# Layer norm in token rows: statistics during the scan, one VectorE pass per quad at the end

## Chip, core and metric

The kernel runs on one core of a Trainium2 chip. The metric is device microseconds (us) of one execution; the time of a kernel is the median of its runs.

## What is computed

B = 32 sequences of T = 64 tokens with D = 512 features, in float32. A GRU runs over the tokens (its first state is `cond`) and is added to x; then a layer takes sums of 8 tokens as blocks (8 per sequence), scores and mixes them, projects the mix, adds it to every token and normalises; the result is added once more.

```
h_t = gru_cell(h_{t-1}, x_t);          x1 = x + h            # 64 steps in sequence
block_n = sum of x1 over 8 tokens;     keys = block_n @ Wk^T, scaled to unit rms, * rms_weight
attn = softmax(keys . q);              att = sum_n attn_n * block_n      # one row per sequence
proj = att @ Wo^T;                     u = x1 + proj
out = x1 + (u - mean(u)) / sqrt(var(u) + eps) * gamma + beta
```

## The kernel before

Layouts. "Recurrence layout": partition = 32 j + b, with j a quarter of the features (128 columns) and b the sequence; a tile [128, 128] is one token of all sequences. A quad is 4 tokens; there are 16. Five instruction streams are written out by hand, one per engine, ordered by semaphores.

Start. SP loads the biases, the first quad of x, then `w_ih` and `w_hh` in four pieces each, each piece after an earlier one has landed. TensorE adds the first four tokens' input products into four PSUM banks as pieces land.

Scan, 64 steps: the first 8 and the last 8 written out, the rest in a hardware loop of 8. A step: 16 recurrent products (L618), each 32 stationary columns into its own 32 partitions; ScalarE's sigmoid (L475) and two tanh (L484); VectorE's cell (L839 to L760), which ends in three transpositions into `h_t` that TensorE's next product waits for. TensorE meanwhile runs the input chunk for five steps ahead (`gi_chunk`, L581), which VectorE takes out (`keep_gi`, L738) and an SP transfer (`move_gi`, L240) brings into recurrence layout; ScalarE lays it into PSUM for the next step (L444). At step 2 of a quad ScalarE and VectorE split the next x into two parts (`split_x`). Behind the cell VectorE does the quad's share: `quad_sum` (x1 = x + h, L768), `quad_partial_sums`, `quad_centre` with TensorE's mean (L604, L778) into `cx_all`, `quad_steps_sum`, and per block `block_sum`. GpSimd adds beta to x1 into `xb_all` (L366). In the last 8 steps there are no chunks from step 59 on; TensorE makes the keys of blocks 0 to 6, SP loads the constants (`load_consts`, L254) and VectorE waits for them at step 60 (L887).

After the scan: scores, softmax, last block's key, and the projection `cp` (centred, one row per sequence, L970). Then the end: `cp` is added to all of `cx_all` (by VectorE L1030, GpSimd L401, and for the last quads by TensorE into PSUM, L701, L702), ScalarE and VectorE square and sum (L534, L976), TensorE sums over the four quarters (L710), the root is refined in five small operations (`refine`), `scale` multiplies by root and gamma (L1009), GpSimd and VectorE add `xb_all` (L406, L1058), SP stores (L320).

## Time and profile before

| | us |
|---|---|
| median of 3 runs | 402.81 (401.72 to 405.34) |
| profiled execution, its time | 404.12 |
| its span, first to last instruction | 402.3 |
| mean granted TensorE clock | 0.961 |

The profile is of one execution. Its page gives busy time by engine and the costliest groups; further views are windows (busy time of each engine in a stretch), the chain of waits (what released each piece of the work that ended last) and timelines. Busy times of TensorE are modelled ends of pipelined products.

### The profile page before, as it was taken

To read this page: it belongs to the slowest core of one execution; us is meant where nothing else is said; L and a number is where in the kernel's file an instruction comes from. 1 tells how busy PE (TensorE), PEld (TensorE's weight loads), DVE (VectorE), ACT (ScalarE), POOL (GpSimd) and SP (SyncE) were. 2 spreads that over 40 slices of the span, in tenths; PEclk is the share of its full clock that TensorE was granted. 3 is DMA by queue.
4 is the path that set the end of the run, shared out by engine and by line. 5 is a ranking of instruction groups with operands and counts; after the bars stand their busy time and mean duration, and the time that the engine had idled before them with its cause. 6 is when DMAs were issued, how large, how long until landed. Compare 5 with 4: busy or idle time off the path is not lost.

```text
span 402.3 us, 9322 instructions
## 1 busy us (share of the span) xinstructions
PE 359.9 (89%) x3102; PEld 212.6 (53%) x3102; DVE 287.7 (72%) x1192; ACT 136.0 (34%) x494; POOL 59.5 (15%) x69
## 2 busy tenths in 40 slices
PE   7999999999999999999999999999999997856300
PEld 4545656565656565656565656565656532623100
DVE  2626767776777677767776777677767667799997
ACT  4502232323232323232323232323234543446532
POOL 3012101010101010101010101010101010263563
PEclk9999999999999999999999999999999999896955
DMA  6956525222222222222222222222221230000234
GB/s 231 399 215 134 174 64 170 66 69 65 66 63 67 62 66 63 67 62 66 63 67 62 66 63 67 63 65 63 67 63 42 65 93 26 2 0 1 104 157 156
DMA packets 18368, 35.46 MB, mean 88 GB/s; under 512 B 1940, under 2 KB 10652, under 8 KB 18348
## 3 DMA queue, kind: packets, MB, share of 16 engines
q1 hardware_dynamic: 18268, 35.15, 29.3%
q8 instruction: 10, 0.16, 0.2%
q0 software_dynamic: 80, 0.07, 0.1%
q14 instruction: 10, 0.08, 0.1%
HBM read 19.21 MB, written 4.19 MB: 58 GB/s over the span
## 4 chain that ended last, share of the span: by engine, by line
PE 73%; DVE 15%; DMA 8%; SPq 1%; issue 1%; POOL 1%; ACT 0%; DVEq 0%; POOLq 0%
PE gates_ps L618 38%; PE gi_ps L581 32%; DVE cx_all L1009 5%; DMA xb_all<-in_w_ih_dram 3%; DVE cx_all L1030 2%; DMA w_hh<-in_w_hh_dram 2%; DMA gamma<-in_gamma_dram 2%; DMA cx_all<-in_b_hh_dram 1%; DVE cx_all L1058 1%; PE third_ps L682 1%; PE third_ps L618 1%; DVE w_hh L1001 1%; PE fourth_ps L618 1%; DVE w_hh L995 1%; DVE cx_all L1025 1%
## 5 line engine op out<-in xcount | busy, mean ns | idle before, releaser
L618 PE MATMUL gates_ps<-w_hh,h_t 128*32 128x384 f32 x1920 | 167.3, 489 | 2.4 <-DVE h_t L760 2.1
L618 PEld LDWEIGHTS gates_ps<-w_hh,h_t 128*32 128x32 f32 x1920 | 56.7, 109 | 84.5 <-issue 54.4
L581 PE MATMUL gi_ps<-w_ih_hi,xt_hi 128*128 128x384 f32 x240 | 86.8, 362 | 0.0
L475 ACT ACTIVATE rz<-gates_ps 128x256 f32<-128x256 f32 x60 | 23.0, 384 | 171.3 <-PE gates_ps L618 171.3
L581 PE MATMUL gi_ps<-w_ih_lo,xt_hi 128*128 128x384 f32 x240 | 80.9, 337 | 0.0
L581 PE MATMUL gi_ps<-w_ih_hi,xt_lo 128*128 128x384 f32 x240 | 80.7, 336 | 0.0
L839 DVE TENSOR_TENSOR rz<-gates_ps,rz 128x128 f32<-128x128 f32 x60 | 17.5, 292 | 80.2 <-ACT rz L475 80.2
L581 PEld LDWEIGHTS gi_ps<-w_ih_hi,xt_hi 128*128 128x128 f32 x240 | 45.0, 188 | 37.5 <-issue 36.8
L366 POOL TENSOR_TENSOR xb_all<-x,beta 128x512 f32 (+1 forms) x16 | 21.2, 1322 | 175.9 <-DVE x L768 175.9
L581 PEld LDWEIGHTS gi_ps<-w_ih_lo,xt_hi 128*128 128x128 f32 x240 | 45.1, 188 | 0.0
L581 PEld LDWEIGHTS gi_ps<-w_ih_hi,xt_lo 128*128 128x128 f32 x240 | 45.1, 188 | 0.0
L760 DVE STREAM_TRANSPOSE h_t<-hist 128x32 f32<-128x32 f32 x189 | 36.5, 217 | 2.4 <-issue 0.2
L754 DVE TENSOR_TENSOR hist<-zh,n 128x32 f32<-128x32 f32 (+1 forms) x192 | 34.2, 201 | 2.2
L738 DVE TENSOR_TENSOR gi_tok<-gi_ps,b_in 128x384 f32<-128x384 f32 x60 | 33.1, 551 | 2.0 <-POOL b_in L380 1.5
L747 DVE SCALAR_TENSOR_TENSOR n<-rz,n 128x32 f32<-128x32 f32 (+1 forms) x192 | 31.0, 189 | 0.0
L484 ACT ACTIVATE n<-n 128x32 f32<-128x32 f32 (+1 forms) x128 | 28.9, 256 | 3.8 <-DVE n L844 3.8
L435 ACT ACTIVATE gates_ps<-bhh_n 128x128 f32<-128x128 f32 x60 | 16.9, 281 | 21.5 <-DVE rz L839 21.5
L444 ACT ACTIVATE gates_ps<-gi 128x256 f32<-128x256 f32 x60 | 22.5, 375 | 1.9 <-DMA gi<-gi_tok 0.3
L844 DVE TENSOR_TENSOR n<-rz,gi 128x32 f32<-128x32 f32 x120 | 21.6, 222 | 0.0
L406 POOL TENSOR_TENSOR cx_all<-cx_all,xb_all 128x1024 f32<-128x1024 f32 x7 | 17.5, 2501 | 16.4 <-DVE cx_all L1009 15.4
L372 POOL COPY br_all<-br_cur 128x128 f32 x7 | 2.0, 289 | 100.0 <-DVE br_turned L792 100.0
L784 DVE TENSOR_REDUCE bs<-x 128x128 f32<-128x512 f32 x15 | 16.1, 1074 | 0.0
(197 smaller groups left out, 332.7 us busy)
## 6 DMA issues: line engine op xcount, KB each, us to landing
gi<-gi_tok SPq DMA_DIRECT2D x60, 192.0 KB, 3.3
x<-in_x_rec_dram SPq DMA_DIRECT2D x16, 256.0 KB, 2.8
x_t<-in_x_t_dram SPq DMA_DIRECT2D x15, 256.0 KB, 3.2
out_dram<-cx_all SPq DMA_DIRECT2D x7, 512.0 KB, 2.6
xb_all<-in_w_ih_dram SPq DMA_DIRECT2D x4, 768.0 KB, 6.9
w_hh<-in_w_hh_dram SPq DMA_DIRECT2D x4, 768.0 KB, 7.9
wo_t<-in_wo_t_dram SPq DMA_DIRECT2D x1, 1024.0 KB, 5.4
wk_t<-in_wk_t_dram SPq DMA_DIRECT2D x1, 1024.0 KB, 5.5
```

The lines of the kernel that those rows point to most:

```text
L366: pool.tensor_tensor(xb_all[:, bass.ds(quad * Q, Q), :], x1[:], over_steps(beta), ALU.add).then_inc(xb_ready, 1)
L444: act.activation(gates_ps[:, P:3 * P], gi[:, (s // Q) % 2, first + P:first + G3], ACT.Copy).then_inc(seeded, 1)
L475: act.activation(rz[:], gates_bank(t)[:, P:3 * P], ACT.Sigmoid).then_inc(rz_ready, 1)
L484: act.activation(n[:, c], n[:, c], ACT.Tanh).then_inc(n_ready, 1)
L581: mm = pe.matmul(gi_ps[tok][:, 0:G3], a[:, k, :], w[:, k, gi_cols(j)], start=(k == 0 and a is xt_hi and w is w_ih_hi), stop=(k == NJ - 1 a ...
L618: mm = pe.matmul(gates_bank(t)[j * B:(j + 1) * B, P:], h_t[:, k * B:(k + 1) * B], chunk(w_hh, k, j), start=False, stop=(k == NJ - 1), skip ...
L738: dve.tensor_tensor(gi_tok[:, tok, :], gi_ps[tok][:, 0:G3], b_in[:, gi_cols(j)], ALU.add).then_inc(gi_tok_ready, 1)
L747: dve.scalar_tensor_tensor(out=n[:, c], in0=z[:, c], scalar=1.0, in1=n[:, c], op0=ALU.subtract, op1=ALU.mult).then_inc(terms_ready, 1)
L754: dve.tensor_tensor(hist[:, s, c], zh[:, c], n[:, c], ALU.subtract).then_inc(h_ready, 1)
L760: dve.transpose(h_t[:, c], hist[:, s, c]).then_inc(ht_ready, 1)
L844: dve.tensor_tensor(n[:, c], r[:, c], i_n[:, c], ALU.add).then_inc(n_pre_ready[number], 1)
L1009: ins = dve.scalar_tensor_tensor(out=cx_all[:, c * C + t, :], in0=u_of(c, t), scalar=rstd[:, c * C + t:c * C + t + 1], in1=gamma[:], op0=A ...
```

## The change

x1 is kept twice: feature-major in `x1t` [feature, quad, 4, (b, step)], as x arrives for the input products, with the turned state added in place; and token-major in `gcx` [(b, step), quad, 512], where the state comes through `h_tok`, four SP transfers a quad from `hist`. With a token's 512 features in one row, ScalarE takes its mean and its sum of squares with accumulators at step 2 of a quad (`token_stats`), VectorE centres and multiplies by gamma (`centre_tokens`); ScalarE adds beta to `x1t` (`add_beta`). The variance of u = x1 + cp is s2 + 2 x1.cp + |cp|^2: after `cp` TensorE makes the middle term for all tokens (`cross_sums`), VectorE picks each token's own sequence, GpSimd raises to the power -0.5, TensorE lays the root out by token. TensorE transposes x1 + beta of each quad into a PSUM bank (`lay_x1`) and adds root times gamma times cp (`add_gcp`, 32 contraction rows each, by quad another 32 rows of the array); VectorE's `finish` is gcx * root + bank, and SP stores each quad. GpSimd's beta add, TensorE's quad mean, the squares, `refine`, `scale` and the adds of `cp` and x go. Constants are loaded at the start through the ScalarE queue and spread by TensorE (`lay_pick`). `score_keys` moves into the last cell. The last block is summed in turned form.

The core of the diff, blank lines left out:

```diff
+        keys_wq, b_of_tok, last_hs, last_part = b_in[:, 0:D], b_in[:, D:D + P], b_in[:, D + P:D + 2 * P], b_in[:, D + 2 * P:D + 3 * P]
+        gmask = b_in[:, 2 * D:3 * D].rearrange("p (j u) -> p j u", j=NJ)
...
+            def move_h(quad, slot, j):
+                if j == 0:
+                    wait(sp, x1t_ready, quad + 1)
+                    wait(sp, x1_ready, quad)
+                sp.dma_start(h_tok[:, j * P:(j + 1) * P], hist[j * B:(j + 1) * B, slot * Q:(slot + 1) * Q, :]
+                             ).then_inc(h_tok_in, 16)
...
                     if not (last and i * S + s + 5 >= T):
                         move_gi(i, s)
-                    if last and s == 2:
-                        load_consts()
+                    if s % Q == Q - 1 and not (last and s == S - 1):
+                        for j in range(NJ):
+                            move_h(i * 2 + s // Q, s // Q, j)
             def load_w_ih(k):
...
             load_w_ih(0)
             sp.dma_start(hist[:, S - 1, :], cond_d).then_inc(h0_in, 16)
             load_w_ih(1)
             load_w_ih(2)
+            load_w_ih(3)
+            load_x_t(1)
             sp.wait_ge(w_ih_in[0], 16)
-            load_w_ih(3)
-            load_ahead(1)
+            load_w_hh(0)
             sp.wait_ge(w_ih_in[1], 16)
-            load_w_hh(0)
+            load_w_hh(1)
             sp.wait_ge(w_ih_in[2], 16)
-            load_w_hh(1)
+            load_w_hh(2)
             sp.wait_ge(w_ih_in[3], 16)
-            load_w_hh(2)
...
+            for j in range(NJ):
+                if j == 0:
+                    sp.wait_ge(h_ready, 3 * T)
+                    sp.wait_ge(x1_ready, NQ - 1)
+                sp.dma_start(h_tok[:, j * P:(j + 1) * P], hist[j * B:(j + 1) * B, Q:S, :]).then_inc(h_tok_in, 16)
+            for quad in range(NQ):
+                sp.wait_ge(out_ready, quad + 1)
+                sp.dma_start(out[:, quad, :], gcx[:, quad, :]).then_inc(out_stored, 16)
...
-            pool.wait_ge(cp_ready, 1)
-            for c in (2, 3, 5):
-                v = cx_all[:, c * S:(c + 1) * S, :]
-                pool.tensor_tensor(v, v, over_steps(cp, S), ALU.add).then_inc(u_pool, 1)
-            for c in range(NB - 1):
-                pool.wait_ge(scaled, c + 1)
-                v = cx_all[:, c * S:(c + 1) * S, :]
-                pool.tensor_tensor(v, v, xb_all[:, c * S:(c + 1) * S, :], ALU.add).then_inc(out_pool, 1)
+            for part, owns in enumerate(parts_i):
+                cols = slice(owns[0] * Q, (owns[-1] + 1) * Q)
+                pool.wait_ge(var_ready, part + 1)
+                pool.tensor_tensor(rstd[:, cols], var[:, cols], half[:, 0:Q * len(owns)], ALU.pow
+                                   ).then_inc(rstd_ready, 1)
...
+            def token_stats(quad, trash=third_ps[:]):
+                wait(act, x1_ready, quad + 1)
+                act.activation(trash, gcx_of(quad), ACT.Copy, scale=-1.0 / D, accum_out=column(x_mean, quad)
+                               ).then_inc(mean_ready, 1)
+                wait(act, mean_ready, quad + 1)
+                act.activation(trash, gcx_of(quad), ACT.Square, bias=column(x_mean, quad),
+                               accum_out=column(s2_tok, quad)).then_inc(s2_ready, 1)
+            def add_beta(quad):
+                if isinstance(quad, int) and quad == NQ - 1:
+                    act.wait_ge(pre_step, 1)
+                else:
+                    wait(act, part_ready, quad + 1)
+                tile = x1t_of(quad)
+                for k in range(NJ):
+                    ins = act.activation(tile[:, k, :], tile[:, k, :], ACT.Identity,
+                                         bias=beta_t[:, k * B:k * B + 1])
+                ins.then_inc(beta_added, 1)
...
+            act.wait_ge(cp_ready, 1)
+            act.wait_ge(last_sq_ready, 1)
+            act.activation(cp_sq, cp, ACT.Square, accum_out=cp_sums[:, 0:1]).then_inc(cp_squared, 1)
+            act.wait_ge(gcp_laid, 1)
+            act.activation(gcp_all, gates_ps[:], ACT.Copy).then_inc(gcp_kept, 1)
+            token_stats(NQ - 1, stats_trash)
+            for part, owns in enumerate(parts_i):
+                cols = slice(owns[0] * Q, (owns[-1] + 1) * Q)
+                if part == 1:
+                    act.wait_ge(s2_laid, 2)
+                    move_s2(NQ - Q, Q, fourth_ps, 4 * Q)
+                act.wait_ge(rstd_laid, part + 1)
+                act.activation(rstd_tok[:, cols], fourth_ps[:, P + owns[0] * Q:P + (owns[-1] + 1) * Q],
+                               ACT.Copy).then_inc(rstd_kept, 1)
...
+                if first and s == 0:
+                    lay_pick(small_ps, 2)
...
+            def lay_x1(quad):
+                bank = out_ps[quad % len(out_ps)]
+                if quad == NQ - 1:
+                    pe.wait_ge(x1t_ready, NQ)
+                if quad >= len(out_ps):
+                    pe.wait_ge(out_ready, quad - len(out_ps) + 1)
+                elif bank is gates_ps:
+                    pe.wait_ge(gcp_kept, 1)
+                elif bank is cross_ps[1]:
+                    pe.wait_ge(cross_step, 4)
+                v = bank[:].rearrange("p (j k u) -> p k j u", j=NJ, k=NJ)
+                for k in range(NJ):
+                    pe.matmul(v[:, k], x1t[:, quad, k, :], ident[:], is_transpose=True, start=(k == 0), stop=False,
+                              skip_group_check=True)
...
+            def cross_sums(part, i):
+                bank, col = cross_ps[part], parts_i[part].index(i) * P
+                for k in range(NJ):
+                    for g in range(Q):
+                        mm = pe.matmul(bank[g * B:(g + 1) * B, col:col + P], cp_t[:, k * B:(k + 1) * B],
+                                       x1t[:, i * Q + g, k, :], start=(k == 0), stop=(k == NJ - 1),
+                                       skip_group_check=True)
+                if i == parts_i[part][-1]:
+                    mm.then_inc(cross_laid, 1)
+            def lay_rstd(part):
+                pe.wait_ge(rstd_spread, part + 1)
+                for i in parts_i[part]:
+                    mm = pe.matmul(fourth_ps[:, P + i * Q:P + (i + 1) * Q], rstd_of[:, i * P:(i + 1) * P],
+                                   own_n[:], start=True, stop=True, skip_group_check=True)
+                mm.then_inc(rstd_laid, 1)
+            def add_gcp(i):
+                pe.wait_ge(gcp_kept, 1)
+                for g in range(Q):
+                    rows = slice(g * B, (g + 1) * B)
+                    pe.matmul(out_ps[(i * Q + g) % len(out_ps)][:], rstd_of[rows, i * P:(i + 1) * P],
+                              gcp_all[rows, :], start=False, stop=True, skip_group_check=True,
+                              tile_position=(g * B, 0)).then_inc(u_laid, 1)
+            pe.wait_ge(cp_t_ready, 1)
+            cross_sums(0, 0)
+            pe.wait_ge(cp_squared, 1)
+            pe.wait_ge(cp_beta_ready, 1)
+            pe.matmul(fourth_ps[:, 0:2], same_b[:], cp_sums, start=True, stop=True).then_inc(cp_summed, 1)
+            pe.wait_ge(gcp_ready, 1)
+            pe.matmul(gates_ps[:], same_b[:], gcp_own, start=True, stop=True).then_inc(gcp_laid, 1)
+            cross_sums(1, 1)
+            pe.wait_ge(cp_const_ready, 1)
+            lay_rstd(0)
+            add_gcp(0)
+            pe.wait_ge(s2_split, 2)
+            pe.wait_ge(rstd_kept, 1)
+            lay_s2(NQ - Q, Q, fourth_ps, 4 * Q)
+            pe.wait_ge(cross_step, 2)
+            pe.wait_ge(x1t_ready, NQ)
+            cross_sums(2, 2)
+            cross_sums(2, 3)
+            for quad in range(Q, 2 * Q):
+                lay_x1(quad)
+            pe.wait_ge(s2_moved, 2)
+            lay_rstd(1)
+            add_gcp(1)
+            pe.wait_ge(rstd_kept, 2)
+            lay_rstd(2)
+            for i in (2, 3):
+                for g in range(Q):
+                    lay_x1(i * Q + g)
+                add_gcp(i)
         @block.vector
         def _(dve):
             def split_x(quad):
                 wait(dve, x_hi_ready, quad)
-                dve.tensor_tensor(xt_lo[:], x_t[:], xt_hi[:].bitcast(F32), ALU.subtract).then_inc(x_lo_ready, 1)
+                dve.tensor_tensor(xt_lo[:], x1t_of(quad), xt_hi[:].bitcast(F32), ALU.subtract).then_inc(x_lo_ready, 1)
             def keep_gi(idx, pos):
...
-                dve.transpose(h_t[:, c], hist[:, s, c]).then_inc(ht_ready, 1)
...
+            def add_turned(quad, slot):
+                wait(dve, ht_ready, quad * (3 * Q) + 3 * Q + 3)
+                tile = x1t_of(quad).rearrange("p k (b t) -> p (k b) t", t=Q)
+                dve.tensor_tensor(tile, tile, turned[:, slot * Q:(slot + 1) * Q, :].rearrange("p t c -> p c t"),
+                                  ALU.add).then_inc(x1t_ready, 1)
+            def sum_steps(quad, slot):
+                dve.tensor_reduce(parts_t[:, slot, :], x1t_of(quad).rearrange("p k (b t) -> p (k b) t", t=Q), AX.X,
+                                  ALU.add).then_inc(part_ready, 1)
+            def add_tokens(quad):
+                wait(dve, x_tok_in, (quad + 1) * 16)
+                wait(dve, h_tok_in, (quad + 1) * (16 * NJ))
+                dve.tensor_tensor(gcx_of(quad), gcx_of(quad), h_tok[:], ALU.add).then_inc(x1_ready, 1)
+            def centre_tokens(quad):
+                wait(dve, s2_ready, quad + 1)
+                dve.scalar_tensor_tensor(out=gcx_of(quad), in0=gcx_of(quad), scalar=column(x_mean, quad),
+                                         in1=gamma_tok[:], op0=ALU.add, op1=ALU.mult).then_inc(gcx_ready, 1)
...
+                if last and s == S - 1:
+                    score_keys()
...
                 if not (last and t + 5 >= T):
                     keep_gi(t + 5, s + 5)
                 if tt == 2 and not last:
                     split_x(quad + 2)
-                if peeled and s < 3:
+                if tt == Q - 1:
+                    add_turned(quad, slot)
...
+                if tt == 0:
+                    sum_steps(quad - 1, 1 - slot)
+                if tt == 1:
+                    add_tokens(quad - 1)
+                if tt == 2 and slot == 0:
                     block_sum(i - 1)
+                if tt == Q - 1:
+                    centre_tokens(quad - 1)
+                if last and s == 3:
+                    dve.tensor_reduce(step_of_tok[:], ident[:].rearrange("p (b t) -> p t b", t=Q), AX.X, ALU.add
+                                      ).then_inc(step_made, 1)
                 if last and s == 4:
-                    dve.wait_ge(consts_in, 16 * 5)
-                    dve.tensor_tensor(wq[:], wq[:], q_row, ALU.mult).then_inc(wq_ready, 1)
-                    dve.tensor_tensor(wq_rec[:], wq_rec[:], q_row_rec, ALU.mult).then_inc(wq_ready, 1)
+                    dve.tensor_reduce(last_part, x1t[:, NQ - 1].rearrange("p k (b t) -> p (k b) t", t=Q), AX.X,
+                                      ALU.add).then_inc(pre_step, 1)
+                    split_s2(0, NQ - Q)
                 if last and s == 5:
...
                 if last and s == 6:
-                    sum_ahead()
-                    score_keys()
...
-                dve.wait_ge(scaled, NB + number)
-                dve.tensor_tensor(v, v, xb_all[:, steps, :], ALU.add).then_inc(out_dve, 1)
+            dve.transpose(cp_t, cp).then_inc(cp_t_ready, 1)
+            dve.tensor_tensor_reduce(cp_beta, cp, beta_rec, -2.0, 0.0, ALU.mult, ALU.add, cp_sums[:, 1:2]
+                                     ).then_inc(cp_beta_ready, 1)
+            dve.wait_ge(gmask_made, 1)
+            dve.tensor_tensor(gcp_own.rearrange("p (j u) -> p j u", j=NJ), gmask,
+                              cp[:, None, :].broadcast_to([P, NJ, P]), ALU.mult).then_inc(gcp_ready, 1)
...
+            def cross_part(part):
+                owns = parts_i[part]
+                cols = slice(owns[0] * Q, (owns[-1] + 1) * Q)
+                size = len(owns)
+                own = cross_own[:, 0:size * P]
+                dve.wait_ge(cross_laid, part + 1)
+                wait(dve, cross_step, 2 * part)
+                dve.tensor_tensor(own.rearrange("p (i c) -> p i c", i=size),
+                                  cross_ps[part][:, 0:size * P].rearrange("p (i c) -> p i c", i=size),
+                                  tok_of_b[:, None, :].broadcast_to([P, size, P]), ALU.mult).then_inc(cross_step, 1)
+                dve.wait_ge(cross_step, 2 * part + 1)
+                dve.tensor_reduce(cross[:, cols].rearrange("p (i t) -> p i t", i=size),
+                                  own.rearrange("p (i b t) -> p i t b", i=size, t=Q), AX.X, ALU.add
+                                  ).then_inc(cross_step, 1)
+                dve.wait_ge(cross_step, 2 * part + 2)
+                dve.wait_ge(s2c_ready, min(part, 1) + 1)
+                dve.scalar_tensor_tensor(out=var[:, cols], in0=cross[:, cols], scalar=2.0 / D, in1=s2c[:, cols],
+                                         op0=ALU.mult, op1=ALU.add).then_inc(var_ready, 1)
+            def spread_rstd(part):
+                owns = parts_i[part]
+                cols = slice(owns[0] * Q, (owns[-1] + 1) * Q)
+                size = len(owns)
+                dve.wait_ge(rstd_ready, part + 1)
+                dve.tensor_tensor(rstd_of[:, owns[0] * P:(owns[-1] + 1) * P].rearrange("p (i b t) -> p i b t", i=size, t=Q),
+                                  tok_of_b[:].rearrange("p (b t) -> p b t", t=Q)[:, None].broadcast_to([P, size, B, Q]),
+                                  rstd[:, cols].rearrange("p (i t) -> p i t", i=size)[:, :, None].broadcast_to([P, size, B, Q]),
+                                  ALU.mult).then_inc(rstd_spread, 1)
+            def finish(quad):
+                dve.wait_ge(gcx_ready, quad + 1)
+                dve.wait_ge(u_laid, quad + 1)
+                dve.wait_ge(rstd_kept, (1, 2, 3, 3)[quad // Q])
+                dve.scalar_tensor_tensor(out=gcx[:, quad, :], in0=gcx[:, quad, :], scalar=rstd_tok[:, quad:quad + 1],
+                                         in1=out_ps[quad % len(out_ps)][:], op0=ALU.mult, op1=ALU.add
+                                         ).then_inc(out_ready, 1)
...
+            add_const(0, Q)
+            cross_part(0)
+            centre_tokens(NQ - 2)
+            spread_rstd(0)
+            centre_tokens(NQ - 1)
+            split_s2(NQ - Q, NQ)
+            for quad in range(2):
+                finish(quad)
+            dve.wait_ge(s2_moved, 2)
+            add_const(Q, NQ)
+            cross_part(1)
+            finish(2)
+            spread_rstd(1)
+            finish(3)
+            cross_part(2)
+            finish(4)
+            spread_rstd(2)
+            for quad in range(5, NQ):
+                finish(quad)
 def kernel(**inputs):
```

## Rows read from the trace of the kernel before

**Rows 1.** Page, part 1: busy us of each engine (share) xinstructions.

```profile
PE 359.9 (89%) x3102; PEld 212.6 (53%) x3102; DVE 287.7 (72%) x1192; ACT 136.0 (34%) x494; POOL 59.5 (15%) x69
```

**Rows 2.** Windows: stage, its us, busy of each engine (xcount), PE clock, DMA share, GB/s.

```profile
0.00:27.36 27.36, 23.98 (x199) 13.50 (x199) 11.36 (x24) 10.70 (x14) 3.81 (x22) 1.00 0.80 308
27.36:319.65 292.29, 292.14 (x2581) 177.62 (x2580) 207.06 (x955) 90.00 (x310) 24.61 (x31) 1.00 0.28 74
319.65:347.60 27.95, 23.91 (x190) 10.31 (x190) 19.51 (x95) 11.14 (x32) 2.56 (x4) 0.99 0.15 44
...
355.60:402.30 46.70, 14.22 (x32) 6.84 (x32) 43.59 (x106) 20.67 (x125) 25.86 (x10) 0.70 0.23 90
```

**Rows 3.** Chain of waits in the scan: start us, us, what.

```profile
57.82 2.72 PE gates_ps L618 x32
...
62.83 2.72 PE gates_ps L618 x32
...
67.95 2.72 PE gates_ps L618 x32
```

**Rows 4.** Timeline, scan, VectorE and ScalarE: start, us, instruction [idle before <-releaser].

```profile
197.04 0.29 DVE L839 TENSOR_TENSOR rz<-gates_ps,rz 128x128 f32<-128x128 f32 x1 [1.28 <-ACT rz L475]
...
207.05 0.29 DVE L839 TENSOR_TENSOR rz<-gates_ps,rz 128x128 f32<-128x128 f32 x1 [0.95 <-ACT rz L475]
...
201.63 0.38 ACT L475 ACTIVATE rz<-gates_ps 128x256 f32<-128x256 f32 x1 [2.12 <-PE gates_ps L618]
...
314.74 0.61 ACT L458 ACTIVATE wo_t<-wo_t 128x512 f32<-128x512 f32 x1
```

**Rows 5.** Timeline of the last steps: TensorE, VectorE, ScalarE.

```profile
336.05 2.79 PE L618 MATMUL gates_ps<-w_hh,h_t 128*32 128x384 f32 x32 [1.94 <-DVE h_t L760]
...
344.94 0.16 DVE L826 TENSOR_TENSOR score<-key_dot,key_rms 128x2 f32<-128x2 f32 x1 [0.79 <-POOL key_rms L393]
...
343.78 0.38 ACT L475 ACTIVATE rz<-gates_ps 128x256 f32<-128x256 f32 x1 [2.33 <-PE gates_ps L618]
```

**Rows 6.** Timeline from the last block's turned sum to cp: VectorE, GpSimd, VectorE.

```profile
347.30 0.31 DVE L928 STREAM_TRANSPOSE br_turned<-br_cur 128x128 f32<-128x128 f32 x1
...
352.74 0.56 POOL L396 TENSOR_TENSOR w_hh<-w_hh,half 128x1 f32<-128x1 f32 x1 [2.27 <-DVE w_hh L945]
...
355.29 0.29 DVE L970 TENSOR_SCALAR w_hh<-w_hh 128x128 f32<-128x128 f32 x1
```

**Rows 7.** Groups by line: out<-in xcount | busy us, mean ns | idle before.

```profile
L1030 DVE TENSOR_TENSOR cx_all<-cx_all,w_hh 128x512 f32<-128x512 f32 x4 | 8.9, 2296 | 0.0
...
L778 DVE SCALAR_TENSOR_TENSOR cx_all<-small_ps,x 128x512 f32 (+1 forms) x16 | 10.8, 677 | 0.0
```

**Rows 8.** Chain of waits, start and one later transfer issue on SP.

```profile
1.06 0.50 DVE xb_all L903
...
1.57 0.39 SPq L290
...
320.61 0.55 SPq L240
```

**Rows 9.** Timeline of TensorE after the last block.

```profile
352.99 1.08 PE L675 MATMUL gi_ps<-wo_t,w_hh 128*32 128x128 f32 x32 [0.53 <-DVE w_hh L948]
...
357.52 1.02 PE L701 MATMUL third_ps<-cx_all,ident 128*128 128x512 f32 x2
...
358.37 1.02 PE L702 MATMUL third_ps<-w_hh,ident 128*128 128x512 f32 x2
...
366.10 0.58 PE L710 MATMUL small_ps<-w_hh,same_b 128*128 128x16 f32 x2 [6.71 <-DVE w_hh L976]
...
366.52 2.06 PE L701 MATMUL gi_ps<-cx_all,ident 128*128 128x512 f32 x2
```

**Rows 10.** Page, part 6: DMA issues xcount, KB each, median us to landing.

```profile
gi<-gi_tok SPq DMA_DIRECT2D x60, 192.0 KB, 3.3
```

**Rows 11.** Timeline of VectorE, its last instruction.

```profile
399.08 0.69 DVE L1058 TENSOR_TENSOR cx_all<-cx_all,xb_all 128x512 f32<-128x512 f32 x1
```

669 lines of the change are left out of this document (288 added, 381 removed).

## Prediction

> **What bounds the kernel now.** I read the page first: TensorE is busy for 359.9 us (89% of the span), VectorE for 287.7 [rows 1]. A share over the whole span mixes stages, so the windows come next [rows 2]. There are five. A start of 27.4 us with the DMA engines 80% busy; 292 us of scan in which TensorE is never idle; 28 us of last steps; 8 us in which the attention comes down to one projection `cp`; and 46.7 us of layer norm in which VectorE is busy for 43.6 and TensorE for 14.2. The change rewrites the last stage and moves work from it into the second.
>
> The scan's period is TensorE's own. In the chain of waits a recurrent product (2.72) and an input chunk (the rest) follow each other, 5.01 from product to product, and 5.12 where the mean of a quad (L604) is laid between them [rows 3]. VectorE waits 1.28 us for the sigmoid in one step of a quad, 0.95 us in its fullest one, and ScalarE waits 2.12 us for the gates after `split_x` [rows 4]. These gaps are what the added work must fit into.
>
> In the last steps two gaps open: TensorE waits 1.94 us for a state that is late because VectorE and ScalarE stood before constants that the SP queue loads late, and VectorE waits 0.79 us for GpSimd's power before the last cell [rows 5]. From the last block's turned sum (347.61) to `cp` (355.58) it is 8.0 us [rows 6]. The end is VectorE's chain: it begins with four adds of `cp` at 2.30 us each while GpSimd adds beside it, where the same size of pass costs 0.68 in L778, with GpSimd mostly quiet [rows 7]; squares, roots, scalings and the adds of x follow it, step by step.
>
> **Removed and added, in order of time.**
>
> *Start.* One more memset (0.50, less 0.08 of overlap with its neighbour) precedes `bias_made`, and SP issues one more small load first (its neighbour takes 0.39; I take 0.35, an estimate) [rows 8]. DMA sets this stage, so all weights land 0.8 us later. w_ih 3 and w_hh 0 to 2 are issued sooner, but the last, w_hh 3, still waits for w_ih 3: I credit nothing, at best 1.3 us. The constants' products on TensorE (some 2 us) lie under those loads. `lay_pick(small_ps, 2)` does not: it stands after the first step's input chunk, four float32 products of 128 columns, a quarter of 0.85 each [rows 9], 0.85 together. Some 0.2 us that the second step waits behind `b_in` go, as the load of `b_hh` shrinks by a third. Sum +1.4.
>
> *Scan.* `quad_mean` goes from TensorE: (5.12 - 5.01) x 14 = -1.5. VectorE gets, by step of the quad, the steps' sum, the token add, nothing new, and the turned add plus centring (0.68 for each pass of 512 columns, as L778 [rows 7]): the sizes that it had, in another order, so it keeps about 1 us of gap. ScalarE gets two passes over 512 columns with accumulators (0.61 each [rows 4], some 0.3 for the read-out and the wait between them: 1.5, an estimate) in the gap of 2.12, and four bias adds of 128 columns, about 1.1, in a gap of 3 us. What is queued behind `token_stats` is the sigmoid, so its margin is 0.6 us, the smallest there is. GpSimd loses its add of beta. SP issues four more transfers (`move_h`) a quad behind the chunk move of step 3. They wait for `add_turned`, then 4 x 0.55 to issue [rows 8] and 3.3 to land [rows 10], 5.5 in all; `add_tokens` needs them two steps (10 us) later and the `hist` rows are overwritten a quad later. Nothing stalls by these numbers. The price if ScalarE's work runs over: 15 quads times what exceeds 0.6 us.
>
> *Last steps.* Constants are there from the start: -1.9. `score_keys` now stands inside the last cell, behind the adds it once held up: the sigmoid of the last cell ended at 344.16, but VectorE took the scores from 344.94 on and two operations of 0.17 first [rows 5], so -1.1, and +0.35 for these two. The last block is summed already turned: the last state must be turned first, +0.5 (an estimate: three pieces of a quarter to half of the 0.31 us block [rows 6]), and the block's own transposition goes, -0.3. ScalarE carries `square_keys`, `token_stats` and four copies of `s2` before the last sigmoid; that fits with no margin, I add 0.2. End of the turned sum: 347.6 + 1.4 - 1.5 - 1.9 - 1.1 + 0.35 + 0.5 - 0.3 + 0.2 = 345.2; with 0.4 for TensorE's first eight transpositions ahead of the keys, 345.6.
>
> *To `cp`.* The multiply over seven blocks and the reduction behind it become seven operations of 0.30 (as [rows 6] has for 128 columns); that takes work off VectorE but puts `add_tokens(15)` on the path, which waits for four transfers issued from about 344.5 on (2.2 + 3.3: 350.0). I keep 7.3 of the 8.0 us: `cp` at 352.9.
>
> *From `cp` to the first `finish`.* VectorE: turn (0.31), product with beta (0.3), `gcp_own` over 512 columns (0.68), three small ones and a cross part from PSUM (1.4), GpSimd's power (0.56, [rows 6]), the spread (0.3). TensorE in between: 16 column-strip products (1.08 for such a set), a 512-column one (1.02), 16 more, the laid root, the first `add_gcp` [rows 9]. With about 0.06 for each hand-over the chain is 5.9 us: 358.8.
>
> *The sixteen `finish` passes.* Each reads one SBUF tile and one PSUM bank over 512 columns, L778's form: 0.68 busy, about 0.62 apart [rows 7], so 9.9, and 2.8 for the cross parts, spreads and `add_const` between them: 12.7 if VectorE sets it. TensorE has per quad four transpositions, 128 columns each. No row shows one. As full float32 products they cost 4 x 0.21 = 0.85 (a quarter of 0.85 each); if each also waits for its own weights more, I bound it by 1.4, and if a transposition streams faster less, 0.4. I take 0.8; and per four quads one `add_gcp`. Its four products of 512 columns read different rows of the array. One takes 0.85 [rows 9]. The nearest row for shared strips is L618: sixteen products of 384 columns in 2.72 us [rows 3], 0.17 each where one alone streams for about 0.64 (0.85 x 384/512), so four run together. Those are column strips; row strips are in no row. So 0.9 or 3.4; I take 0.9, as that is the row nearest in kind. Then six PSUM banks couple the engines: `lay_x1(15)` waits for `finish(9)`, then transposition, `add_gcp` and four passes follow. Walking it gives the last pass 12.7 to 17.7 us after the first start; I take 15.6. Last pass ends at 374.4.
>
> The store adds what lay between the last pass (399.77) and the end, 2.5 [rows 2, 11]: span 376.9. The profiled execution of before took 404.12 us for its 402.3 us span, 1.8 more, and lies 1.3 over the runs' median of 402.81. So the forecast is 376.9 + 1.8 - 1.3 = 377.4, I say 377 us, 26 us less.
>
> The Trainium skill (TensorEngine Tiling (Array Packing), Key Properties) says that tiles operate independently, row tiles as well as column tiles. By it the four products cost about 0.9, the value taken above; no row here shows it for row tiles.
>
> **Rivals.**
> *A, the forecast* (0.52): VectorE and TensorE share the pace at the end; 371 to 382.
> *B, the row strips take turns* (0.12). For it: no row shows them together. Against: L618's strips. Each `add_gcp` costs 3.4, +2.5 four times: 387. Then the edit's claim, one VectorE pass per quad as the price, is not met: TensorE sets the end.
> *C, the clock falls* (0.12). In the last stage of before the granted clock is 0.70, and a 512-column product that took 1.02 us at the full 2.4 GHz took 2.06 after 6.7 us in which TensorE was idle [rows 2, 9]. The new end keeps TensorE at work, which speaks against it. If half of its 16 us run at 1.2 GHz: +8, 385.
> The Trainium skill (TensorE: Matmul & The Clock Gate, Part 4) says that transpositions do not count as busy for the clock. By it the stretch of 12 quads' transpositions would run at the lower level, which is rival C; no row here has a transposition on TensorE.
> *D, ScalarE's statistics hold up the scan a little* (0.14): over by 0.4 us a quad, 15 x 0.4 = 6: 383.
> *E, better than summed* (0.07): w_hh lands 1.3 sooner and transpositions hide: 371 or less.
> *F, slower than before* (0.03). One mechanism: `token_stats` stands ahead of the sigmoid of step 3. From 0.6 + 26/15 = 2.3 us over its price of 1.5 it eats the whole gain; a pass would have to cost 1.9 us instead of 0.61. At 2.5 us a pass, 15 x (5.1 - 2.1) = 45: 422. No row has such a price.
>
> The range must leave out 2 in 10: 369 to 388 leaves out F, the tail of E and of C. A measurement of this kernel can tell about 1% from no change, so faster means under 398.8. Only F and the rest of D ends there: faster 0.96, same 0.02, slower 0.02.
>
> **What would show it.** Right: the recurrent product and chunk still 5.01 apart, without the 5.12; no 1.94 us gap before the second-last step; `cp` near 353; sixteen passes of 0.68 on VectorE; four `add_gcp` products starting within 0.1 us of each other; last pass near 374. Wrong: a sigmoid that starts over 0.1 us after its gates in step 3 of a quad (D, F); `add_gcp` products 0.85 apart (B); granted clock under 0.9 after `cp` (C); first recurrent product of the second step not at 29.0.

## The result, and the profile of the changed kernel

The changed kernel takes 383.3 us (median of 4 runs, 381.33 to 385.01), the kernel before 402.9 beside it: a ratio of 0.950, interval 0.944 to 0.957, so 5% faster. The forecast was 377 us, range 369 to 388.

The page of the changed kernel, and its windows over the same five stages as before [rows 2]: start, scan, last steps, to `cp`, end.

```profile
PE 363.2 (95%) x3281; PEld 213.9 (56%) x3281; DVE 261.8 (69%) x1134; ACT 159.3 (42%) x506; POOL 20.2 (5%) x53
```

```profile
core 0: us, PE busy (x) PEld busy (x) DVE busy (x) ACT busy (x) POOL busy (x), PEclk, DMA share, GB/s
0.00:28.10 28.10, 25.68 (x211) 15.29 (x211) 12.51 (x28) 11.49 (x16) 7.89 (x30) 1.00 0.76 293
28.10:319.34 291.24, 291.24 (x2557) 173.21 (x2560) 206.50 (x951) 124.92 (x415) 5.42 (x16) 1.00 0.33 86
319.34:344.98 25.64, 23.28 (x190) 9.33 (x190) 18.73 (x94) 18.39 (x57) 2.24 (x4) 1.00 0.11 29
344.98:352.39 7.41, 4.47 (x106) 3.56 (x106) 6.35 (x24) 0.93 (x5) 0.57 (x1) 1.00 0.17 38
352.39:380.50 28.11, 18.53 (x222) 12.48 (x222) 17.74 (x39) 3.61 (x14) 4.10 (x3) 0.88 0.40 151
```

The two profiled spans differ by 21.8 us (402.3 and 380.5). By stage, from the events that bound them in both (they differ by up to 0.1 us from the round windows above): start +0.8, scan -1.1, last steps -2.2, to `cp` -0.7, end -18.6 (46.7 before, 28.1 now). VectorE was busy for 43.6 us of the end and is now for 17.7.

The end in detail. TensorE's timeline of the changed kernel, around the third root; the four products of one `add_gcp` are the lines of 32*128, here the first half of each:

```profile
363.47 0.60 PE L683 MATMUL third_ps<-ident,x1t 128*128 128x128 f32 x4
364.24 0.69 PE L740 MATMUL gates_ps<-w_hh 32*128 32x512 f32 x1
364.25 0.69 PE L740 MATMUL gi_ps<-w_hh 32*128 32x512 f32 x1
364.26 0.69 PE L740 MATMUL first_ps<-w_hh 32*128 32x512 f32 x1
364.26 0.69 PE L740 MATMUL third_ps<-w_hh 32*128 32x512 f32 x1
...
367.97 0.58 PE L731 MATMUL fourth_ps<-own_n,w_hh 128*128 128x4 f32 x4 [2.58 <-DVE w_hh L1080]
368.40 0.63 PE L683 MATMUL small_ps<-ident,x1t 128*128 128x128 f32 x4
```

GpSimd's powers and, on VectorE, what waits for them and for TensorE:

```profile
356.61 1.46 POOL L367 TENSOR_TENSOR w_hh<-w_hh,half 128x4 f32<-128x4 f32 x1 [7.03 <-DVE w_hh L1071]
362.48 1.01 POOL L367 TENSOR_TENSOR w_hh<-w_hh,half 128x4 f32<-128x4 f32 x1 [4.41 <-DVE w_hh L1071]
365.72 1.64 POOL L367 TENSOR_TENSOR w_hh<-w_hh,half 128x8 f32<-128x8 f32 x1 [2.24 <-DVE w_hh L1071]
```

```profile
360.04 0.75 DVE L1090 SCALAR_TENSOR_TENSOR gcx<-gcx,w_hh,first_ps 128x512 f32<-128x512 f32 x1 [0.31 <-issue]
...
367.39 0.42 DVE L1080 TENSOR_TENSOR w_hh<-tok_of_b,w_hh 128x256 f32<-128x256 f32 x1 [1.06 <-POOL w_hh L367]
...
371.49 0.75 DVE L1090 SCALAR_TENSOR_TENSOR gcx<-gcx,w_hh,small_ps 128x512 f32<-128x512 f32 x1 [1.70 <-issue]
...
376.80 0.74 DVE L1090 SCALAR_TENSOR_TENSOR gcx<-gcx,w_hh,gi_ps 128x512 f32<-128x512 f32 x1
```

Read them together: the root of the last eight quads is ready only at 367.4; TensorE stands still for 2.58 us in front of `lay_rstd(2)`, with transpositions queued behind it that need no root; and VectorE pays 1.70 us of that before `finish(8)`. Between the first pass and the end of the last lie 17.5 us, of which the passes themselves are 16 x 0.66 = 10.6.

### The profile page after: what moved, and what is told of

The parts are those of the page before. It is cut to its first block, busy times and chain, and to the rows that moved or that the text cites. A ratio compares the mean times of both kernels' runs of the same rounds, so it can differ in the third digit from the quotient of the medians.

```text
span 380.5 us, 9825 instructions
## 1 busy us (share of the span) xinstructions
PE 363.2 (95%) x3281; PEld 213.9 (56%) x3281; DVE 261.8 (69%) x1134; ACT 159.3 (42%) x506; POOL 20.2 (5%) x53
## 4 chain that ended last, share of the span: by engine, by line
PE 89%; DVE 5%; issue 2%; DMA 1%; POOL 1%; SPq 1%; POOLq 0%; ACT 0%; DVEq 0%
PE gates_ps L595 42%; PE gi_ps L563 36%; DMA h_tok<-hist 1%; DVE gcx L1090 1%; PE first_ps L595 1%; PE first_ps L656 1%; PE fourth_ps L595 1%; PE third_ps L595 1%; PE keys_ps L595 1%; PE fourth_ps L656 1%; PE third_ps L656 1%; PE keys_ps L656 1%; POOL w_hh L367 1%; PE gi_ps L577 0%; PE keys_ps L721 0%
## 5 line engine op out<-in xcount | busy, mean ns | idle before, releaser
L595 PE MATMUL gates_ps<-w_hh,turned 128*32 128x384 f32 x1920 | 167.3, 489 | 0.5 <-DVE turned L808 0.5
L595 PEld LDWEIGHTS gates_ps<-w_hh,turned 128*32 128x32 f32 x1920 | 56.4, 109 | 85.6 <-issue 56.4
L870 DVE TENSOR_TENSOR rz<-gates_ps,rz 128x128 f32<-128x128 f32 x60 | 17.5, 292 | 80.4 <-ACT rz L477 80.4
L808 DVE STREAM_TRANSPOSE turned<-hist 128x32 f32<-128x32 f32 (+1 forms) x192 | 36.7, 217 | 2.2
L443 ACT ACTIVATE x1t<-x1t,beta_t (+1 forms) x64 | 20.1, 387 | 0.0
L814 DVE TENSOR_TENSOR x1t<-x1t,turned 128x512 f32 (+1 forms) x16 | 17.4, 1089 | 0.0
L876 DVE TENSOR_TENSOR zh<-rz,hist 128x96 f32<-128x96 f32 x64 | 16.0, 251 | 0.0
```

Source lines behind the costliest of these rows:

```text
L443: ins = act.activation(tile[:, k, :], tile[:, k, :], ACT.Identity, bias=beta_t[:, k * B:k * B + 1])
L595: mm = pe.matmul(gates_bank(t)[j * B:(j + 1) * B, P:], before[:, k * B:(k + 1) * B], chunk(w_hh, k, j), start=False, stop=(k == NJ - 1), s ...
L808: dve.transpose(turned[:, s, c], hist[:, s, c]).then_inc(ht_ready, 1)
L870: dve.tensor_tensor(r, bank[:, 3 * P:], r, ALU.mult).then_inc(rh_ready, 1)
```

## Experiments

Twelve kernels, each timed against the kernel before on its own chip. Two of them turned out to leave the time alone (`filled` 383.0 us, `act_one` 383.0, the changed kernel 383.3), which shows how far such medians agree. Across chips they agree less: the kernel before took 401.2 to 402.9 us beside these runs, so a difference of 1 us between two medians of different chips says nothing, and the ratios are what to compare.

### What the end of the kernel before consisted of

`before_quiet` cuts GpSimd's adds after `cp` from whole chunks to two columns; the rest of those adds is left out:

```diff
-v = cx_all[:, c * S:(c + 1) * S, :]
-pool.tensor_tensor(v, v, over_steps(cp, S), ALU.add).then_inc(u_pool, 1)
+v = cx_all[:, c * S, 0:2]
+pool.tensor_tensor(v, v, cp[:, 0:2], ALU.add).then_inc(u_pool, 1)
```

(and the same for the adds of `xb_all`).

> The kernel before, with GpSimd's large adds after cp cut to two columns each: three chunks lack cp and seven of eight chunks lack x + beta. Theory (VectorE's and GpSimd's passes slow each other, which is what the layer norm at the end paid for): VectorE's adds of cp go from 2.30 to 0.68 us and its other passes get shorter too, -12 to -20: 383 to 391. Rival (VectorE's passes are that long by themselves): they stay at 2.3 us, and only the tail after the last scaling goes, -2 to -4.

Measured: 382.4 us, ratio 0.953 (0.949 to 0.956), -19 us. VectorE's groups after `cp`, in this kernel and in the kernel before:

```profile
L1009 DVE SCALAR_TENSOR_TENSOR cx_all<-cx_all,w_hh,gamma 128x128 f32<-128x128 f32 x32 | 9.2, 342 | 0.1
L1030 DVE TENSOR_TENSOR cx_all<-cx_all,w_hh 128x512 f32<-128x512 f32 x4 | 2.5, 686 | 0.0
```

```profile
L1009 DVE SCALAR_TENSOR_TENSOR cx_all<-cx_all,w_hh,gamma 128x128 f32<-128x128 f32 x32 | 15.5, 534 | 0.1
```

The mean of an add of `cp` falls from 2296 ns [rows 7] to 686, that of a scaling from 534 to 342. From `cp` to the end it is 27.5 us where it was 46.7. So the theory holds, but the means hide its form. Shortest, median and longest of the same two groups in the kernel before, in ns, and GpSimd beside the first:

```profile
L1030 DVE TENSOR_TENSOR cx_all<-cx_all,w_hh x4: 693/2824/2843, 355.6 to 361.7; 128x512 f32<-128x512 f32 x4
L1009 DVE SCALAR_TENSOR_TENSOR cx_all<-cx_all,w_hh,gamma x32: 252/343/2448, 368.6 to 384.0; 128x128 f32<-128x128 f32 x32
355.66 8.35 POOL L401 TENSOR_TENSOR cx_all<-cx_all,w_hh 128x1024 f32<-128x1024 f32 x3 [2.35 <-DVE w_hh L970]
```

Most scalings take 0.34 us in both kernels. In the whole old end nine VectorE passes are long (three of L1030, three of L1009, one each of L995, L1001 and L1058, 2.3 to 2.8 us), and each of them ends 0.03 to 0.55 us after one of GpSimd's adds ends: a pass that meets a running add stands until the add is over. Against the same forms alone the nine lose 19.0 us together, and the end became 19.2 us shorter. The changed kernel does all the work and takes about what the old one takes with GpSimd's part left out. No run gives GpSimd's adds to VectorE in the old layout; they are 20 passes of 512 columns, at 0.62 each about 12 us (an estimate), so that move alone would have won about 7 of the 19.

### Do the row strips run together?

`one_strip` lets all four products of an `add_gcp` read the first strip:

```diff
-pe.matmul(out_ps[(i * Q + g) % len(out_ps)][:], rstd_of[rows, i * P:(i + 1) * P],
-          gcp_all[rows, :], start=False, stop=True, skip_group_check=True,
-          tile_position=(g * B, 0)).then_inc(u_laid, 1)
+pe.matmul(out_ps[(i * Q + g) % len(out_ps)][:], rstd_of[0:B, i * P:(i + 1) * P],
+          gcp_all[0:B, :], start=False, stop=True, skip_group_check=True,
+          tile_position=(0, 0)).then_inc(u_laid, 1)
```

> The changed kernel (383.3 us), with the four products of each add_gcp reading the same 32 rows of the array instead of four different strips; the quads so take the root of the wrong step, nothing is left out. Theory (row strips run together, which is why an add_gcp costs 1.06 us): now they take turns, 4 x 0.85 = 3.4 us each, +2.35 four times on TensorE, of which up to 2 us hide where VectorE is behind: 390 to 393 us. Rival (the short time comes from the four different PSUM banks, not from the rows): no change, 383.

Measured: 395.4 us, ratio 0.985 (0.982 to 0.988), +12 against the changed kernel. TensorE's timeline:

```profile
371.02 1.02 PE L740 MATMUL gi_ps<-w_hh 32*128 32x512 f32 x2
371.88 1.02 PE L740 MATMUL first_ps<-w_hh 32*128 32x512 f32 x2
372.73 1.02 PE L740 MATMUL third_ps<-w_hh 32*128 32x512 f32 x2
```

They start 0.85 apart; with four strips they start within 0.02 and all are done after 1.1. The theory stands, and the banks, which are the same four in both, are not what counts. The sum is above the 7 to 9.7 expected. In the profiled execution the clock was at 0.50 from 359 to 369, over part of the first `add_gcp`, two of whose products took 1.91 there, and again from 379 to 383; that this makes up the rest is argued, not shown.

### The roots, and the queue behind them

`root_narrow` takes each power over one column and leaves out the roots of the other columns. `order` moves three transpositions ahead; `order_both` also asks for the second and third cross part sooner on VectorE; `cross_first` is `order_both` with `cross_sums(2, 2)` moved ahead of `lay_rstd(0)`. TensorE's part of `order`, which all three have:

```diff
+for g in range(3):
+    lay_x1(2 * Q + g)
 pe.wait_ge(rstd_kept, 2)
 lay_rstd(2)
-for i in (2, 3):
-    for g in range(Q):
-        lay_x1(i * Q + g)
-    add_gcp(i)
+lay_x1(2 * Q + 3)
+add_gcp(2)
+for g in range(Q):
+    lay_x1(3 * Q + g)
+add_gcp(3)
```

VectorE's part of `order_both` (`...` marks what is left out):

```diff
-dve.wait_ge(s2c_ready, min(part, 1) + 1)
+dve.wait_ge(s2c_ready, part + 1)
...
 centre_tokens(NQ - 2)
+add_const(Q, 2 * Q)
 spread_rstd(0)
+cross_part(1)
 centre_tokens(NQ - 1)
 split_s2(NQ - Q, NQ)
 for quad in range(2):
     finish(quad)
+spread_rstd(1)
+finish(2)
 dve.wait_ge(s2_moved, 2)
-add_const(Q, NQ)
-cross_part(1)
-finish(2)
-spread_rstd(1)
+add_const(2 * Q, NQ)
+cross_part(2)
 finish(3)
-cross_part(2)
 finish(4)
 spread_rstd(2)
```

> The changed kernel, with GpSimd's three powers over one column each instead of 4, 4 and 8; the roots of the other columns are left out, so their quads are scaled wrongly. Theory (a power costs 0.42 us and 0.15 more for each column, 0.57 for one): the first at 0.57 instead of 1.46 puts the first finish 0.9 earlier, the third at 0.57 instead of 1.64 shortens TensorE's gap of 2.58 by 1.07; together -1.5 to -2.0, about 381.5. Rival (the power is slow because VectorE runs a 512-column pass beside it): the powers stay over 1 us and the time at 383.

> The changed kernel, with three of the third group's transpositions (lay_x1(8) to (10)) ahead of lay_rstd(2) on TensorE, which waits 2.58 us there for the root. Theory (in the last stage TensorE's queue order costs what VectorE then waits for, 1.70 us before finish(8)): the three fill the gap, the first add of gcp after it comes 1.35 earlier, and so does the end: 381.9, -1.4. Rival (the end is set by the lateness of the third root, not by what stands behind it): within 0.3 of 383.3.

> As the run with the transpositions ahead of lay_rstd(2), and on VectorE the second cross part ahead of the first finish passes and the third ahead of finish(3), so that the second and third root are asked for earlier. Theory (the third root comes from 367.4 to about 365.5, TensorE has no gap left, VectorE's passes of 0.66 follow each other): -2.5 to -3.5 against the changed kernel, 380 to 381. Rival (TensorE's own work per quad sets the end once the gap is filled): no more than -1.4.

> The changed kernel with the transpositions ahead of lay_rstd(2), the cross parts asked for earlier on VectorE, and on TensorE cross_sums(2, 2) (1.08 us) in the 1.5 us in which it waits for the first root. Theory (from the first add of gcp on TensorE is busy without a break and sets the end): 1.0 us less than with the first two edits alone, ratio 0.943 to 0.945, 379 us. Rival (VectorE's passes and the waits for PSUM banks set it by now): within 0.3 us of them, ratio 0.9466.

First and last pass are the starts of the first and the last `finish` in the profiled execution, in us.

| kernel | us | ratio (interval) | first pass | last pass |
|---|---|---|---|---|
| changed kernel | 383.3 | 0.950 (0.944 to 0.957) | 360.04 | 376.80 |
| `root_narrow` | 381.0 | 0.947 (0.944 to 0.949) | 358.83 | 375.81 |
| `order` | 380.2 | 0.946 (0.944 to 0.948) | 359.13 | 374.73 |
| `order_both` | 380.1 | 0.947 (0.944 to 0.949) | 358.30 | 374.23 |
| `cross_first` | 378.4 | 0.941 (0.938 to 0.944) | 359.12 | 372.71 (by 0.66 from 370.73) |

The interval of the changed kernel overlaps those of the first three, so their gains of 1 to 2 us are read from the traces.

The powers of `root_narrow`:

```profile
355.88 0.98 POOL L368 TENSOR_TENSOR w_hh<-w_hh,half 128x1 f32<-128x1 f32 x1 [6.05 <-DVE w_hh L1072]
361.27 0.54 POOL L368 TENSOR_TENSOR w_hh<-w_hh,half 128x1 f32<-128x1 f32 x1 [4.42 <-DVE w_hh L1072]
```

One column 0.54, four 1.01, eight 1.64: about 0.4 and 0.16 for each column, as the theory had it. The first is 0.44 above its like in both kernels (0.98 and 1.46); both stand beside VectorE's centring, a pass with all its tiles in SBUF, the others beside `finish` or a cross part, which read PSUM. In `order_both` the second power comes to stand beside a centring and takes 1.45 instead of 1.01. So the rival was partly right: a fixed 0.44, not the growth.

`order` fills TensorE's wait, and VectorE's wait before `finish(8)` falls from 1.70 to 0.54. Its stretch from first to last pass is 15.6 where it was 16.8, -1.2 of the 1.4 expected; the other 0.9 by which its span is shorter (378.4 for 380.5) lies before the first pass, where its clock did not fall. `order_both` gained nothing measurable on top: its third root is asked for sooner (363.32 instead of 365.72), but TensorE is then busy without a wait of 0.1 us from 357 and the clock was at 0.50 from 359 to 362, which made the cross sums there 3.33 us long instead of 1.96. `cross_first` takes a product set (1.08) out of that stretch; here first to last pass is 13.6, where `order_both` has 15.9 with the fall in it. By the ratios it lies 0.6% under `order_both` (0.941 and 0.947, the intervals apart by a hair) where 1.0 us was expected. That fits the theory that TensorE's own work sets the end, and not the rival. It is the fastest kernel of this study: 378.4 us, by the ratios about 1% under the changed kernel, where the two intervals just touch, at 0.944.

### Does filling the idle time keep the clock?

In the changed kernel's end the granted clock fell. TensorE's timeline, then the same product set in `order`, where that place is unchanged:

```profile
352.78 1.78 PE L721 MATMUL keys_ps<-x1t,w_hh 128*32 128x128 f32 x32 [1.85 <-DVE w_hh L1041]
354.94 1.83 PE L750 MATMUL gates_ps<-w_hh,same_b 128*128 128x512 f32 x2
```

```profile
352.75 1.08 PE L721 MATMUL keys_ps<-x1t,w_hh 128*32 128x128 f32 x32 [1.74 <-DVE w_hh L1044]
```

`filled` puts work into the wait:

```diff
+for _ in range(8):
+    pe.matmul(keys_ps[:], xt_hi[:, 0, :], w_ih_hi[:, 0, 0:D], start=True, stop=True)
 pe.wait_ge(cp_t_ready, 1)
 cross_sums(0, 0)
```

> The changed kernel, with eight products whose result nobody reads (128x128, 512 columns, float32r, about 0.21 us each) in TensorE's idle 1.85 us before the first cross sums. Theory (the clock fell to half from 353 to 356.3 because TensorE was idle from 350.93 to 352.78): the clock stays at 1.00, cross sums take 1.08 instead of 1.78, the 512-column product about 1.02 instead of 1.83, -1.5: 381.8. Rival (the clock falls in any case): the granted clock still 0.5 there and 383.3 or a little more.

Measured: 383.0 us, ratio 0.952 (0.948 to 0.957). At 352 to 356 the clock was full, and the cross sums took 1.08. Windows of `filled`:

```profile
344.00:348.00 4.00, 3.67 (x65) 3.20 (x67) 3.75 (x16) 1.07 (x5) 0.00 (x0) 0.60 0.30 68
...
352.00:356.00 4.00, 4.00 (x72) 2.38 (x70) 2.89 (x11) 1.37 (x4) 0.41 (x1) 1.00 0.02 6
...
368.00:372.00 4.00, 4.00 (x22) 2.17 (x20) 0.84 (x3) 0.00 (x0) 0.00 (x0) 0.58 0.52 197
```

It fell at 345, behind another wait (1.65 us), and at 369, behind the 2.58 us before `lay_rstd(2)`. In `order` it fell nowhere before the last pass, with the waits of 1.65 and 1.74 left as they were. So neither theory holds as stated: in these kernels falls do come behind waits of TensorE of 1.3 to 2.6 us (1.3 in `root_narrow`, 1.5 in `order_both` and `all_three`), but which wait is paid differs from kernel to kernel where the work is the same, and closing one of them bought nothing that can be measured. A wait is not needed either: in `one_strip` the clock fell at 379.2 and at 386.1, and from 363 on TensorE had no wait over 0.05 us; from 369 on its work was transpositions, products of 32 rows one after another and a few of 4 columns. By the traces a fall on the path costs 0.9 us (before the first pass, against `order`) to 1.5 (between first and last pass of `filled`, 18.2 against 16.8); the times of whole executions do not show it: the four of `order` have mean clocks of 0.998, 0.992, 0.994 and 0.988 and took 380.22, 380.22, 380.62 and 379.96 us.

`all_three` is `order_both` with these eight products.

> The changed kernel with the filled idle time before the cross sums, the transpositions ahead of lay_rstd(2) and the cross parts asked for earlier. If the single terms add up, -1.5 and -3: 378.5 to 379.5. Rival (each shows the same wait twice, so that only the larger counts): 380.5.

Measured: 379.6 us, ratio 0.943 (0.940 to 0.946). Below `order_both` by 0.5 us, inside the intervals; the clock fell in it at 358 instead. The terms of the single runs don't add up: the first, -1.5, was not there in `filled` either.

### How much room ScalarE has in the scan

`act_one` and `act_two` put one and two unused passes of 512 columns ahead of each quad's statistics:

```diff
 wait(act, x1_ready, quad + 1)
+if not (isinstance(quad, int) and quad == NQ - 1):
+    act.activation(fourth_ps[:], gcx_of(quad), ACT.Copy)   # act_two: a second one to keys_ps
```

> The changed kernel with one more ScalarE pass over 512 columns (0.58 us, result unused) ahead of each quad's statistics in the scan. Theory (the sigmoid of step 3 has 0.48 us of idle time before it and the turned state 0.28 us before TensorE wants it, 0.76 together): it costs nothing, 383 to 384. Rival, as the prediction priced it (the sigmoid's own gap is the margin): 15 x (0.58 - 0.48) = +1.5, 385.

> The changed kernel with two more such ScalarE passes. Theory (0.76 us of margin): 15 x (1.16 - 0.76) = +6, 389. Rival (0.48 us of margin): 15 x (1.16 - 0.48) = +10, 393.5.

Measured: 383.0 us (ratio 0.951, 0.947 to 0.956) and 387.5 us (0.963, 0.957 to 0.969; two runs). ScalarE's timeline of `act_one`, and TensorE's of `act_two` with the next product:

```profile
201.34 0.19 ACT L434 ACTIVATION_READ_ACCUMULATOR third_ps<-gcx,x_mean  x1
201.48 0.38 ACT L479 ACTIVATE rz<-gates_ps 128x256 f32<-128x256 f32 x1
```

```profile
199.82 2.79 PE L599 MATMUL gates_ps<-w_hh,turned 128*32 128x384 f32 x32
205.08 2.79 PE L599 MATMUL gates_ps<-w_hh,turned 128*32 128x384 f32 x32 [0.17 <-DVE turned L812]
```

In `act_one` the sigmoid still starts with its gates, with nothing left before it, and the time is unchanged. In `act_two` the product of every fourth step comes 5.26 us after the one before instead of 5.02. Two passes add 2 x 0.52 (start to start), 0.24 of it arrives: the margin is 0.80, the sigmoid's idle 0.48 and the slack of the turned state behind it. 15 x 0.24 = 3.6 of the 4.2 us measured.

### The late constants of the kernel before

`before_early` and `before_sooner` move `load_consts()` from the last block's step 2, to the first block's step 6 and to the last block's step 0:

```diff
-if last and s == 2:
+if first and s == 6:   # before_sooner: if last and s == 0:
     load_consts()
```

> The kernel before, with the five loads of the constants moved from the last block to the first one; nothing of the end is changed. Theory (TensorE's wait of 1.94 us in the last steps comes from them): -1.9, ratio 0.995. Rival (another late operation takes its place in the last steps): nothing.

> The kernel before, with the five loads of the constants two steps (10 us) earlier in the last block, behind the chunk move of its first step; the first try, in the first block, put them ahead of the 1 MB load of wk, and TensorE stood still for 4.24 us at 77 us because the chunk moves were stuck behind both. Theory (the late constants cost the last steps 1.9 us): the wait of 1.94 us goes and nothing takes its place, -1.9, ratio 0.995. Rival (two chunk moves of 3.3 us behind the loads' 5.5 us of issue are late themselves): a new wait of VectorE for a chunk move, ratio 1.0 or above.

Measured: 405.5 us, ratio 1.010 (1.007 to 1.013), and 402.7 us, ratio 1.001 (0.999 to 1.004). TensorE's timelines, in this order:

```profile
81.16 4.48 PE L618 MATMUL gates_ps<-w_hh,h_t 128*32 128x384 f32 x32 [4.24 <-DVE h_t L760]
```

```profile
327.06 2.79 PE L618 MATMUL gates_ps<-w_hh,h_t 128*32 128x384 f32 x32 [3.07 <-ACT gates_ps L444]
336.83 2.79 PE L618 MATMUL gates_ps<-w_hh,h_t 128*32 128x384 f32 x32 [0.21 <-DVE h_t L760]
```

and SP's queue in `before_sooner`:

```profile
313.76 2.62 SPq L262 DMA_DIRECT2D gamma<-in_gamma_dram  x1
316.42 0.62 SPq L240 DMA_DIRECT2D gi<-gi_tok  x1
```

The 1.94 us wait of [rows 5] is gone in both (0.2 is left), but a new one has come: the five loads take 5.7 us to issue (310.73 to 316.38), and the chunk moves behind them are late; in `before_early` the 1 MB load of wk stood there as well. For the first place neither expectation held (a new wait came, but in the scan, and with the clock down over the product behind it), for the second the rival did. The wait of 1.94 does come from these loads, but neither of the two other places for them on SP made the kernel faster. The changed kernel loads four short rows at the start, spreads them with TensorE, and does not have the wait; no run makes that move alone.

## Why the prediction was right, and where it was off

The mechanism was right: a scan that keeps its period, an end of one VectorE pass per quad, 5% faster. The number alone would not show it, since 383.3 is just what rival D priced (383); the traces do, with the scan's products 5.02 apart in every step and ScalarE's gap still open. The prediction also read the old end as passes of 2.30 us each; they are one of 0.69 and three of 2.8 that stood behind GpSimd. Nothing in its sum hung on that, but it is why the old end was so long. Step by step:

- **Start, +1.4: was +0.8.** The first step's product began at 22.2 (21.0 before), `lay_pick` took 0.89 as said, but the stall before the last part of w_hh, credited with nothing at 1.3 at best, went: the product of the second step began at 28.1. (The 29.0 of the prediction's signs does not follow from its own sum, 27.4 + 1.4 = 28.8.)
- **Scan, -1.5: was -1.1.** Products are 5.02 apart throughout, the 5.12 is gone. Passes that I called of the same size were not: the strided add of the turned state takes 1.09 us, the steps' sum 0.68. They are not in the same step, and VectorE's smallest gap is 0.63, not about 1. ScalarE's smallest was 0.48 (0.6 forecast), its true margin 0.80 (`act_one`, `act_two`): there was more room against rival D than the prediction had counted.
- **Last steps: right.** The turned sum ended at 345.1 (345.2 to 345.6); the misses of the start (-0.6) and of the scan (+0.4) nearly cancel in it, which is luck. As said, ScalarE had no margin: `move_s2` ended at 341.78 and the sigmoid began at 341.89. The wait of 1.94 before the second-last product is gone.
- **To `cp`: 352.4 (352.9).** The transfers landed at 349.5 (350.0) and cost VectorE 0.43.
- **`cp` to the first pass, 5.9: was 7.65.** The term that was mis-sized is GpSimd's power. I took 0.56 from a power over one column; over four, beside a centring, it takes 1.46 (`root_narrow`). The other 0.9 is the clock at 0.50 over the cross sums, which `order` did not have (6.8, with the power at 1.46 in it).
- **The passes, 15.6: was 17.5.** A pass takes 0.66 start to start, not 0.62 (16 x 0.04 = 0.6), and the third power 1.64, not 0.56 (1.1), with transpositions queued behind it; `order` takes 1.2 us of this back. The transposition was over-priced: 0.44 a quad, not 0.8.
- **`add_gcp`, 0.9: was 1.06,** against 3.4 in turn. `one_strip` shows that this would have given 395: rival B counted +10 on a forecast of 377, and +12 came on 383.
- **Store 2.9, not 2.5.** These last four give +4.1, `cp` gives -0.5: the span is 380.5, not 376.9. The rest of the 6.3 us by which the median missed is the step from one execution to the median (I took 1.3 off as in the kernel before; this profiled run lies 1.0 under its own median) and 0.4 of rounding.

Two of the prediction's signs of being wrong did show: the second step did not begin at 29.0, and the clock after `cp` was 0.88, under the 0.9 named for rival C. But rival C had the wrong shape. The clock was 1.00 in the transposing stretch from 360 to 376; it was at 0.50 from 353.0 to 356.4, which cost 0.9 us, and again from 376.9 on, when TensorE had finished. The Trainium skill's rule that transpositions don't count as busy (TensorE: Matmul & The Clock Gate, Part 4) did not show in this execution; in `filled` a fall at 369 did stand behind a wait and a transposing stretch. The falls of `one_strip` at 379 and 386 stand behind no wait; what came before them was transpositions mixed with products that use 32 rows at a time, and no run here takes those two apart.

## To carry over

Before pricing a stage that two engines share, look for the same form of pass with and without the neighbour: here 19 of 47 us were nine VectorE passes standing behind GpSimd's adds. Look at the shortest and the longest of a group, not at its mean, to see whether all passes are slow or a few are waiting. Price a small operation by its column count, not by its name, and wherever it is on the path ask what stands behind it in the queue that needs nothing from it. A load that is cheap in bytes can cost more in issue time on a queue than the wait it was to remove.

## What the hardware showed that I had not expected

- A VectorE pass with two SBUF tiles as inputs and a GpSimd add with two take turns, each as a whole: the one that starts second stands until the first is over. A pass with a PSUM tile goes on beside the add. From the end of the kernel before, VectorE and GpSimd:

```profile
384.48 1.13 DVE L1009 SCALAR_TENSOR_TENSOR cx_all<-gates_ps,w_hh,gamma 128x128 f32<-128x128 f32 x4
...
386.80 0.63 DVE L1025 TENSOR_TENSOR cx_all<-cx_all,gamma 128x512 f32<-128x512 f32 x1
387.34 2.31 DVE L995 TENSOR_TENSOR w_hh<-w_hh 128x16 f32<-128x16 f32 x1
...
386.80 2.82 POOL L406 TENSOR_TENSOR cx_all<-cx_all,xb_all 128x1024 f32<-128x1024 f32 x1
...
395.74 2.71 DVE L1058 TENSOR_TENSOR cx_all<-cx_all,xb_all 128x512 f32<-128x512 f32 x1
```

  GpSimd adds from 384.44 to 386.79, from 386.80 to 389.62 and from 395.18 to 397.90. The four passes with a PSUM tile run beside the first at 0.26 start to start, as without it. Then VectorE's L1025 and GpSimd's second add start together: L1025 takes its usual 0.63, the add takes 2.82 where one that VectorE doesn't cross takes 2.34 (390.54), and the next VectorE pass, of 16 columns, which takes 0.17 alone, ends at 389.65, just behind the add. The last line takes 2.71 beside the third add and 0.69 alone [rows 11].

  The Trainium skill (GPSIMD Engine Reference, Specifications) says that GpSimd shares its SBUF interfaces with VectorE and contends with instructions that have two SBUF inputs. By it exactly these passes suffer; the trace agrees.
- A float32 transposition of 128x128 on TensorE costs 0.11 us in a row of sixteen (four in 0.44), against 0.21 for a product of that size (a quarter of 0.85 for 512 columns).
- A power on GpSimd: 0.54, 1.01 and 1.64 us over one, four and eight columns of 128 partitions, and 0.44 more where a VectorE pass over SBUF tiles was already running.
- A `dma_start` that spreads one row or four over 128 partitions occupied SP for 0.5 to 2.8 us.
